# Table products as pairs of 64-row tiles in four PSUM banks, and their places in TensorE's order

## The reference

```python
h = _ln(x, n1g[l], n1b[l])
xi, xj = (h[dst], h[src])
q  = (xi @ Wq[l] + bq[l]);   kn = (xj @ Wkn[l] + bkn[l]);   vn = (xj @ Wvn[l] + bvn[l])
...   # ke, ve from the edge features; softmax of q * (kn + ke) over the edges of a node
agg = jax.ops.segment_sum(msg, dst, num_segments=n)
gate = jax.nn.sigmoid(agg @ Wih[l] + bih[l] + h @ Whh[l] + bhh[l])
upd = agg + gate * (h @ Wself[l] + bself[l] - agg)
x = x + upd @ Wout[l] + bout[l]
x = x + _mlp(_ln(x, n2g[l], n2b[l]), mW1[l], mb1[l], mW2[l], mb2[l])
```

## Time and profile before

| | us |
|---|---|
| median of 3 runs | 8777.02 (8776.52 to 8793.31) |
| profiled execution, its own time | 8783.83 |
| its span in the profile | 8781.8 |
| stretch ahead of the first layer, to the first gather | 2232 to 2332.58 |
| first stretch between layers, to the first gather | 4306.8 to 4494.64 |
| second stretch between layers, to the first gather | 6468.9 to 6654.35 |

### The profile page before, as it was taken

One profiled execution on the slowest core, in us unless ns is written; L12 is line 12 of the kernel. 1 busy time (PEld: TensorE's weight loads), 2 busy tenths in 40 slices (PEclk: granted clock), 3 DMA queues, 4 the chain that ended last, 5 costly groups with the idle time before them and its releaser, 6 DMA issues.

```text
span 8781.8 us, 45085 instructions
## 1 busy us (share of the span) xinstructions
PE 3106.8 (35%) x9968; PEld 1796.7 (20%) x9968; DVE 5809.3 (66%) x6415; ACT 2858.1 (33%) x2225; POOL 6378.1 (73%) x6734
## 2 busy tenths in 40 slices
PE   2555555554322232222342222222243222323224
PEld 1111111111222222221122121112222222222212
DVE  1766767676577766677656667777655777666775
ACT  1666666666122222222222222222232222222223
POOL 6777777776777777777667777777757777777774
PEclk9877777777666666566566666566666566666566
DMA  3555555554444444444244444444424444444442
GB/s 54 194 198 181 181 181 184 186 191 159 134 142 137 147 138 134 134 135 143 93 136 134 134 134 140 137 142 146 134 70 141 142 137 147 139 134 134 135 134 73
DMA packets 402651, 1245.04 MB, mean 142 GB/s; under 512 B 193381, under 2 KB 251190, under 8 KB 357670
## 3 DMA queue, kind: packets, MB, share of 16 engines
q0 software_dynamic: 215104, 429.19, 18.1%
q1 hardware_dynamic: 166758, 466.07, 15.2%
q10 hardware_dynamic: 20736, 349.23, 10.0%
HBM read 806.18 MB, written 437.84 MB: 142 GB/s over the span
## 4 chain that ended last, share of the span: by engine, by line
POOL 67%; issue 23%; PE 3%; DVE 3%; DMA 1%; DVEq 1%; ACT 1%; POOLq 0%; SPq 0%; ACTq 0%
POOL G L599 66%; POOL s2exp L618 1%; POOL S L605 1%; PE PS L890 0%; PE PS L901 0%; DVE S L1767 0%; PE PS L866 0%; PE PS L859 0%; PE PS L860 0%; DMA G<-xTd 0%; POOL G L644 0%; PE PS L844 0%; PE PS L873 0%; PE PS L811 0%; DVE SXt L1935 0%
## 5 line engine op out<-in xcount | busy, mean ns | idle before, releaser
L599 POOL DMA_INDIRECT G<-tabkv,srcI x4704 | 4438.4, 944 | 1446.6 <-issue 1446.6
L834 PE MATMUL PS<-Wkvp,EA 128*128 128x256 f32 x4704 | 1646.2, 524 | 4229.0 <-DVE PX L1986 4144.9
L834 PEld LDWEIGHTS PS<-Wkvp,EA 128*128 128x128 f32 x4704 | 1236.3, 270 | 4638.2 <-DVE PX L1986 4307.2
L599 POOL DMA_INDIRECT G<-tab,srcI x1568 | 1481.2, 945 | 508.6 <-issue 501.3
L1221 ACT ACTIVATE QQ<-QQ 128x3584 f32<-128x3584 f32 x84 | 539.4, 6421 | 3140.4 <-DVE PX L1986 3027.0
L1983 DVE TENSOR_TENSOR PS<-PS,G 128x512 f32<-128x512 f32 x588 | 408.6, 695 | 1512.3 <-DMA G<-tabkv,srcI 1506.1
L1240 ACT ACTIVATE S<-SXt 128x4480 f32<-128x4480 f32 x81 | 663.6, 8193 | 1236.8 <-DVEq L1997 1236.8
L1942 DVE TENSOR_TENSOR_SCAN SXt<-PS,SXt 128x456 f32<-128x456 f32 (+2 forms) x783 | 765.4, 1051 | 12.4
L1968 DVE TENSOR_TENSOR_SCAN QQ<-PS,QQ 128x456 f32<-128x456 f32 x672 | 679.6, 1084 | 114.2 <-ACT QQ L1221 100.1
L1986 DVE TENSOR_TENSOR PX<-PS,QQ 128x512 f32<-128x512 f32 x588 | 625.0, 1063 | 43.8
L754 PE MATMUL PS<-hid,W2raw 128*64 128x512 f32 x1568 | 479.0, 712 | 334.6 <-ACT hid L1060 325.8
(11 more groups left out here) (360 smaller groups left out, 4079.3 us busy)
## 6 DMA issues: line engine op xcount, KB each, us to landing
st<-S ACTq DMA_DIRECT2D x81, 2240.0 KB
EA<-eaT SPq DMA_DIRECT2D x84, 1792.0 KB, 7.8
QQ<-qexp SPq DMA_DIRECT2D x84, 1792.0 KB
st<-S ACTq DMA_DIRECT2D x27, 3668.0 KB
G<-tabkv,srcI POOLq DMA_INDIRECT x4704, 2.5
xe<-in_edge_attr SPq DMA_DIRECT2D x28, 1792.0 KB
qexp<-zeros SPq DMA_DIRECT2D x28, 1792.0 KB, 10.8
eaT<-eaC ACTq DMA_DIRECT2D x28, 1792.0 KB
```

What stands on the lines that cost most here:

```text
L599: nc.gpsimd.indirect_dma_start(out=G[:, u, t, :], out_offset=None, in_=tab[:, :], in_offset=IND(ap=srcI[:, u, t:t + 1], axis=0)).then_inc( ...
L834: last = mm(PS[:, b + j // 2, 2 * P * (j % 2):2 * P * (j % 2) + 2 * P], EA[:, u, 4 * s + j, :], Wkvp[:, :], start=True, stop=True)
```

## The change

Each table tile becomes two products of 64 rows by 192 columns, one for each half of the partitions, without the zero blocks of `Wqkv`, and each goes to a bank of its own: the pair of tiles 2n and 2n + 1 has banks 0 and 1, or 2 and 7. TensorE waits for free banks, and VectorE for finished tiles, only at even tiles. The spreads of the first half move from bank 7 to bank 6 (in the last layer, which makes no tables, they stay in 7), and with them comes a wait for their root ahead of `turned(l, 6)`, which writes bank 6. The order of TensorE changes: tiles 0 to 3 stand ahead of the first half's spreads, 4 to 7 between the gates and the outputs, 8 to 11 between the variances and the hidden products, 12 to 15 behind the fold.

```diff
-SBANK = (7, 7, 7, 3, 4, 5, 6)
+SBANK = (6, 6, 6, 3, 4, 5, 6)
+CLOSE_SBANK = (7, 7, 7, 3, 4, 5, 6)
+TBANK = ((0, 1), (2, 7))
...
+        def table_part(i, q):
+            return PS[:, TBANK[i // 2 % 2][q], 3 * D * (i % 2):3 * D * (i % 2) + 3 * D]
...
-                    if i >= 3:
+                    if i >= 4 and i % 2 == 0:
                         hold(pe, waits_pe, t_dve, m * NTILE + i - 2)
                     c = BLK[k][0] + j * P
-                    mm(PS[:, i % 3, 0:6 * D], x[:, c:c + P], Wqkv[:, :], start=True, stop=True).then_inc(t_pe, 1)
+                    for q in range(2):
+                        rows, cols = slice(q * D, (q + 1) * D), slice(3 * D * q, 3 * D * (q + 1))
+                        last = mm(table_part(i, q), x[rows, c:c + P], Wqkv[rows, cols], start=True, stop=True)
+                    last.then_inc(t_pe, 1)
...
-            tiles(0, range(0, 11), xT0)
+            tiles(0, range(0, 12), xT0)
             pe.wait_ge(u_copy, len(HALVES[0]))
+            pe.wait_ge(s_act, 1)
             turn_nodes(HALVES[1], UBANK)
-            tiles(0, range(11, 12), xT0)
             pe.wait_ge(u_copy, HALVES[1].start + 1)
-            tiles(0, range(12, 15), xT0)
+            tiles(0, range(12, 16), xT0)
             spreads(0, HALVES[1], sq0)
             pe.wait_ge(u_copy, NB)
-            tiles(0, range(15, NTILE), xT0)
+            tiles(0, range(16, NTILE), xT0)
...
-                tiles(l + 1, range(0, 3), ready=l)
+                tiles(l + 1, range(0, 4), ready=l)
                 spreads(l + 1, HALVES[0])
                 turned(l, 5)
+                hold(pe, waits_pe, s_act, (l + 1) * (1 + len(HALVES[1])) + 1)
                 turned(l, 6)
                 for k in HALVES[1]:
                     gates(l, k)
-                tiles(l + 1, range(3, 4))
+                tiles(l + 1, range(4, 8), ready=l)
                 for k in HALVES[1]:
                     output(l, k)
-                tiles(l + 1, range(4, 6), ready=l)
                 variances(l, HALVES[1])
-                tiles(l + 1, range(6, 11), ready=l)
+                tiles(l + 1, range(8, 12), ready=l)
                 hidden(l, 1, 0)
-                tiles(l + 1, range(11, 12))
                 hidden(l, 1, 1)
                 folded(l, 1)
-                tiles(l + 1, range(12, 15), ready=l)
+                tiles(l + 1, range(12, 16), ready=l)
                 spreads(l + 1, HALVES[1])
-                tiles(l + 1, range(15, NTILE), ready=l)
+                tiles(l + 1, range(16, NTILE), ready=l)
...
                 for i in tiles_of(k):
-                    dve.wait_ge(t_pe, m * NTILE + i + 1)
+                    if i % 2 == 0:
+                        dve.wait_ge(t_pe, m * NTILE + min(i + 2, NTILE))
                     for q in range(2):
                         t = 2 * i + q
-                        part = PS[:, i % 3, 3 * D * q:3 * D * (q + 1)]
+                        part = table_part(i, q)
```

12 lines of the change are left out of this document (6 added, 6 removed).

## The result

The changed kernel takes **8766.60 us** (median of 22 runs, 8760.91 to 8771.23) where the kernel before takes 8778.74 (22 runs, 8772.88 to 8793.31): the ratio is 0.9985 with an interval of 0.9979 to 0.9990. That is 12.1 us less, 0.14%, within the 0.2% that was called no change, and inside the range of 8753 to 8773. The forecast was 8761.6, so the time is 5.0 us above it: the gain is 3.3 us smaller than forecast, and the kernel before is 1.7 us slower over 22 runs than over the three that the forecast started from. The profiled execution took 8761.68, its span is 8758.8.

A forecast was written before the change was run, and what follows sets the result against it. GpSimd's serial indirect gathers were taken as the bound, with savings in the stretches between layers: 6.5 + 0.1 + 0.7 + 0.4 = 7.7 us a boundary, 15.4 for both. 8777.0 - 15.4 = 8761.6 us, range 8753 to 8773.

The forecast's parts named there:

- The first mix: VectorE's first mix after tables 0 to 3, between layers: starts 5.3 us earlier, at 4406.5 instead of 4411.81.
- The hidden start: TensorE's hidden products, second half: start 6.5 us earlier, 20.4 us after the first table evacuation instead of 27.0.
- Rival A: TensorE granted 1.2 GHz at the hidden products: costs 2.1 us a boundary, gain 11.2 in all, 8766 us; chance 0.17.
- A clock of 0.5 at the hidden products: Sign that the forecast is wrong: hidden products running at a granted clock of 0.5 in the changed profile.
- A pair of tiles: TensorE's 64-row table products run side by side: 0.34 us a tile, 0.65 if the halves did not overlap.
- Rival B: The two array halves don't overlap, tiles at 0.65 us: gain 5.4 a boundary, 10.8 in all, 8766 us; chance 0.08.
- The saving behind the fold: After the fold, four tiles in 1.4 us replace three in 2.0 ahead of the spreads: 0.7 us a boundary.
- The 0.1 for tile 11: Tile 11 no longer stands between the two hidden passes on TensorE: 0.1 us a boundary.
- Six register computations: On VectorE from tile 12 on, the wait computations at odd tiles go: 6 x 0.07 = 0.4 us a boundary.
- Mean squares taken as unchanged: TensorE's mean squares behind the tables: 8.39 us taken as unchanged, with bounds of -3.1 and +2.2.
- GpSimd's slack: GpSimd's 6.14 us without work ahead of the second layer's first gather: claimed to stay.
- Mode changes of the array: Drains at tiling-mode changes on TensorE: at most 0.14 us each, 0.6 a boundary, a sum of 14.2 instead of 15.4.

The follow-up runs named there:

- experiment 1: Kernel before with a fourth bank for table products and tile 3 moved ahead of the gates, full-array tiles, a wait at every tile: 8761.61 us, ratio 0.9981.
- experiment 7: Kernel before with only the fourth bank for table products, tile 3 still behind the gates: 8773.48 us, ratio 0.9996.
- experiment 5: Changed kernel with tiles 8 and 9 each issued twice between layers, filling TensorE's pause ahead of the hidden products: 8766.10 us, ratio 0.9985.
- experiment 10: Changed kernel with early mean squares, two unused products behind the first half's variances, and tiles 8 and 9 issued twice; other chip: 8762.33 us, ratio 0.9967.
- experiment 6: Changed kernel with the mean squares in banks 3 to 6, one ahead of each pair of tiles from tile 16 on: 8758.02 us, ratio 0.9978.
- experiment 9: Changed kernel with two unused 512-column products behind the first half's variances, filling the pause there; other chip: 8774.01 us, ratio 0.9980.
- experiment 2: Changed kernel, same order and waits, but each tile one full-array product of 384 columns in a bank of its own: 8777.40 us, ratio 0.9997.
- experiment 8: Changed kernel with tiles 0 to 11 as full-array products and only tiles 12 to 24 as 64-row pairs: 8763.71 us, ratio 0.9985.
- experiment 3: The changed kernel run again without any edit: 8768.68 us, ratio 0.9988.

## Why the prediction was right, and what of it was not

- **The first mix, 5.3 us a stretch.** Right. Predicted 4.8 us from evacuation to mix, measured 4.59 and 4.60 (10.05 and 9.87 before). Experiments 1 and 7 show the cause: with tile 3 moved it is 4.74, with the bank alone 9.36.
- **The hidden start, 6.5.** Predicted 20.4, measured 20.11 and 20.12 instead of 26.96 and 26.68, so 6.85 and 6.56. The outputs ran at full clock (1.00 over 4406.50 to 4411.00).
- **Rival A came in part.** The clock over 4417.7 to 4422.4 is 0.64 and the pass from hidden to fold took 1.1 us longer, where the rival had priced 2.1. A clock of 0.5 at the hidden products was also named as a sign of being wrong, and for 2 us it was there. With the pause filled the pass took 10.82 or 10.83 us in all four stretches of experiments 5 and 10; unfilled, with the same order and tiles, it took 11.7 to 12.0 in six of eight and 10.82 in two (experiments 6 and 9). So the pause makes the slow pass likely and does not fix it.
- **A pair of tiles.** Predicted 0.34 us a tile, measured 1.50 / 4 = 0.375; four full-array tiles in the same place took 2.69. Rival B (no overlap) falls. The saving behind the fold was priced 0.7 and measured 2.04 - 1.50 = 0.54, of which 0.43 reached the root of block 3 (9.06 and 8.63). The 0.1 for tile 11 between the hidden passes was nothing: the whole pass takes 10.83 us with the tile there (experiment 1) and without it (experiment 2).
- **Six register computations, 0.4.** Right in price, and mostly lost again. The price of one is 0.07 us: experiment 1, with a wait for each tile, has 4.74 us from evacuation to mix, the kernels with waits at even tiles 4.59 and 4.60, and two computations lie between. Behind the fold six of them are 0.42, but from root to mean squares the step shrank by 0.14 and 0.13 only. The other 0.29 is one idle time of VectorE, between the root of block 5 and its first tile: 0.53 us in the rows above, 0.24 in the kernel before. It is not a wait for TensorE's products, though TensorE's pairs ran at 1.2 GHz there (0.50 over 4446 to 4455.2): the pair of tiles that follows the idle time ran on TensorE from 4446.07 and had ended at 4446.07 + 1.65 = 4447.72. The idle time is the same in both stretches, in the second profile of the changed kernel and in experiments 2, 5, 6 and 8, and the kernels with a wait at each tile have 0.24. So it belongs to the changed program; what in it stays open.
- **Mean squares taken as unchanged.** They came 0.99 and 0.84 us shorter by the clock (20.07 and 20.16 against 21.06 and 21.00), inside the bounds. The kernel before has 19.98 and 19.97 there in its second profile: it is chance, not the change. This made up for rival A's 1.1, so B came out at 7.58 and 7.14 for a forecast of 7.7 by luck in part: two errors against each other.
- **GpSimd's slack.** Taken to stay at 6.14 us; it fell to 4.62 (in the second stretch from 5.18 to 4.32). Counted from the evacuation, its last scatter came 6.06 us earlier and the first gather 7.58. It was still not the bound; in experiment 6 it became it. Ahead of the first layer the first gather starts at 2332.72 instead of 2332.58, as forecast.
- **Mode changes of the array.** Behind the last gate product, which starts at 4404.67, the 64-row tiles start 0.32 us later; in experiment 2 full-array tiles start 0.22 us behind the same product (4406.89 and 4407.11). So the change costs about 0.1 us there. On the path it does not show: the hidden products start 20.11 us behind the evacuation with 64-row tiles and 20.23 and 20.22 with full-array ones (experiments 2 and 8). The Trainium skill, TensorEngine Tiling (Array Packing), Key Properties, speaks of a drain at such a change; the trace agrees with a small one, and decides for the higher sum.
- **The time.** 15.4 us were forecast. B gave 14.7 in the profiled executions, the medians 12.1, and the repetition of experiment 3 10.3. The measured 8766.6 is also where rivals A and B were priced (8766), so the time alone would not tell them from the forecast; the rows above do. The step that failed is that what lies outside the path of the change was taken to be equal in both kernels. A, which the change touches nowhere ahead of its last few microseconds, varies between 90.2 and 94.9 us; it is 90.2 to 91.2 where the first half's hidden pass is 6.04 or 6.05, 91.3 to 92.4 where it is 7.0 to 7.1, and 93.3 to 94.9 where it is 8.1 to 8.3. The last part of A, from fold to evacuation, is 12.88 us in the changed kernel and in the short stretch of the kernel before alike, so the change's own work there is not the cause. How often a kernel falls in the one or the other differs (experiment 2's eleven runs: eight near 8777.5, three near 8770), and what decides it stays open; experiment 9 could not settle it. So does why experiment 1, whose B is 2.2 and 2.1 us longer, has a median 5 us below that of the whole change, and 7 us below it in their common lot; the two intervals overlap. Its second profile, with a B of 85.85 us in one stretch, leaves it possible that its usual B is nearly that of the change.

## What to carry to other kernels

When an engine waits in program order for one small item behind a long run of others, move that item alone first: one tile brought 70% of what the change brought in its stretches and no less in the whole time, and the extra bank only made it possible. Ask of each block of work what it truly waits for. The mean squares stood behind the tables by their banks alone, and moving them was worth another 4.8 us a stretch, about 8 us in the medians (20 below the kernel before of its lot, for 12.1), up to the point where GpSimd's own scatters took over. A gain of a microsecond won by keeping TensorE busy at one place may not reach the time (experiment 5), so read the whole stretch to the first gather, and compare several profiled executions before a difference under 0.1% is laid to an edit.

## What the runs showed of the hardware

- The same pass of 24 products, behind the same pause of 3.54 us, took 6.02 us in one profile and 8.26 in another, at granted clocks of 1.00 and 0.61. Stretches with the slow pass have an A of 93.3 to 94.9 us, those with the fast one 90.2 to 91.2. The pass itself is 2.0 to 2.3 us of that; the rest lies ahead of it and behind it and was not taken apart.
- One chip changed between two kernels of one lot: 4704 gathers from 4438.3 to 4445.5 us, 1.5 ns each; the 1568 gathers of the first layer went from 1481.6 to 1484.0. The kernel before took 8791.4 there instead of 8778.0, and these two sums are 9.6 us of such a difference. So compare with runs of the same chip and lot, never absolute times.
- Two products of 64 rows in different halves of the array run side by side for 192 columns too: sixteen instructions in 1.50 us at full clock, 0.094 each, where eight full-array ones of 384 columns, for the same four tiles, take 2.69.
- A wait of VectorE on a computed count costs 0.07 us: 4.74 us for four tiles with a wait at each, 4.60 with waits at even tiles only.
